# Four gate parts made during the last scan and brought back with an identity product, and a last product in two halves

## Chip, cores and metric

The kernel runs on one core of a Trainium2 chip. The metric is the device time of one execution in microseconds. Time before: 1269.98 us, the median of three runs (1269.86 to 1270.35).

## What is computed

Two layers act on x, four sequences of 1024 rows of 256 numbers, all in float32. Each layer is modulated by six vectors per sequence (shift, scale and gate of two branches). Layer 0 is a dilated attention and a linear layer whose input is quantised by blocks. Layer 1 is a selective scan (Mamba) and a recurrent gate layer. What matters here is the end of layer 1:

```python
def step(h, inp):                      # the scan, over 1024 rows
    a, bx, c = inp
    h = a * h + bx
    y = jnp.einsum('bds,bs->bd', h, c)
    return (h, y)
...
y = y + D_param[None, None, :] * x_branch
y = y * jax.nn.silu(z)
return jnp.einsum('btd,de->bte', y, c_proj_w)
...
def step(c, xt):                       # the gates, over the 4 sequences
    ft = jax.nn.sigmoid(xt @ wf.T + c @ uf.T + bf)
    it = jax.nn.sigmoid(xt @ wi.T + c @ ui.T + bi)
    gt = jnp.tanh(xt @ wc.T + c @ uc.T + bc)
    c = ft * c + it * gt
    return (c, None)
c_final, _ = lax.scan(step, c0, x)
h = jnp.tanh(jnp.einsum('tbi,oi->tbo', x, wo) + c_final @ uo.T + bo)
```

## The kernel before

The work is cut into G = 8 halves of 512 rows (two per sequence), named h ahead of their scan and g behind it. The scan of a half has 32 steps (STEPS), so the whole program has 256 scan steps, numbered m. The 32 steps are four blocks of channels (kd) of eight steps, and a step holds two states, each 128 channels by 512 rows. For step m:

- ACT makes the decays, two Exp activations of 128x512 into PSUM (`act_decay`, L1254). Banks 0 to 3 hold the states of two steps, so the decays of step m wait for DVE's product of step m - 2.
- POOL multiplies u with the loaded row of B (`pool_scan`, L1914, in odd halves with a small sum at L1920). It waits for the sum of y of step m - 4, whose buffer it takes. SP loads the rows of B and C from DRAM.
- DVE runs the recurrence over both states (`dve_scan`, L1691) and multiplies the result with the row of C (L1697).
- PE adds both halves of that product onto y with the identity (`pe_scan`, L874), in bank Y. After the eighth step DVE multiplies y with silu(z) (`dve_gate`, L1677).

The other work of the halves before and behind goes between the steps. Each engine's program is one list, put together by `in_time`: every chain yields the step at which its next piece is due (tables TIMES, or numbers at the yield), and at each quarter of a step the due pieces are emitted ahead of the scan's own part. An engine runs its list in order, and semaphores join the engines.

A gate of the recurrent layer is a product of 128x512 in two parts: `pe_gate_x` (from hA, the normalised rows; L720) and `pe_gate_c` (from the state c; L728), each two matmuls over k into one PSUM bank. There are six (f, i, c; two blocks of 128 channels each). ACT evicts a gate at L1177 (`act_gate`).

The last half (g = 7) has no scan behind it to hide in, and has chains of its own. `pe_last` makes the projection `c_proj` (L747) in two banks, the parts from c of all six gates, the transposes of the normalised rows (L458), the parts from hA, then the output's products (L784, L735). c for this half is that of half 5 (`c_of(g)`), so it is known long before. The gates' banks are LAST_GATE, and LAST_ORDER is the order in which they are made. ACT and DVE write hA's two blocks (L898 and L1386). `dve_last` has, in order: bias sums for the output (L1632, three times), `dve_sum` (L1615), the gates' arithmetic for either half of c (L1639, L1641, L1645, L1648), and the output sums (L1657 and on). `dve_final` places two more `dve_sum` at L1615 around the last gated product. `act_loads` brings in the rows of earlier halves for the output by DMAs from ACT's queue (L1200, L1203), one every two steps of the last scan.

Of the kernel before, what the change touches and what calls it, by code (L numbers as in the profile page):

```python
# [104 lines left out]
LAST_CPROJ, LAST_GATE, LAST_PX, LAST_OM = (Y0, X0), (X1, 0, 1, 2, 3, Y), (Y0, Y), 0  # L105

LAST_ORDER, LAST_TANH = (0, 2, 4, 1, 3, 5), {1: X0, 2: 2}

# [10 lines left out]
             "ffn_mm", "ffn_tmp", "res1"]  # L119
MAMBA = ["pad", "xb_mm", "xc_init", "conv", "xc", "z_mm", "z_tanh", "z_ev", "bc_mm", "bc_sb", "softplus", "spare",  # L120
         "dt_copy", "u", "dt_cut", "first_decay", "to_add"]
# [17 lines left out]
def build(nc, d):  # L139
    with ExitStack() as ctx:  # L140
# [65 lines left out]
        def cols_view(a):  # L206
# [56 lines left out]
               [rows_view(a) for a in (xb_flat[:, 0:JH * E], xb_flat[:, JH * E:2 * JH * E])] + [woT[:], xrows[(G - 1) % 3]]]  # L263
        gates1 = rowmod

        mod_d = nc.dram_tensor("mod_scratch", (B, 6, E), F32).ap()
# [456 lines left out]

        def pe_gate_c(n, bank, g, first):

            gate, mt = "fic"[n // 2], n % 2
            for k in range(KE):
                x = pe.matmul(ps[:, bank, :], gu[gate][:, k, mt * P:(mt + 1) * P], c_of(g)[:, k, :],  # L728
                              start=(first and k == 0), stop=(not first and k == KE - 1))
            return x  # L730

        def pe_px(q, bank):
            for j in (2 * q, 2 * q + 1):
                for k in range(KE):
                    x = pe.matmul(ps[:, bank, (j % 2) * E:(j % 2 + 1) * E], hA[:, k, j:TH:JH], gw["o"][:, k, :],  # L735
                                  start=(k == 0), stop=(k == KE - 1))
            x.then_inc(S.px_mm, 1)

        def pe_last():
# [4 lines left out]
            def c_proj(kd, q):  # L744
# [4 lines left out]
                return x  # L749

            for q in range(2):

                yield t + 30 + q / 2
                if q == 0:
                    pe.wait_ge(S.gated, 4 * g + KD - 1)
                    pe.wait_ge(S.cp_gated, B)
                    pe.wait_ge(S.px, 2 * g)
                else:
                    pe.wait_ge(S.fin_add, B)
                for kd in range(KD - 1):  # L760
                    c_proj(kd, q)
            yield t + 31.75
            pe.wait_ge(S.c_new, g - 1)
            pe_gate_c(LAST_ORDER[0], LAST_GATE[0], g, True)

            yield t + 32.75
            pe.wait_ge(S.gated, 4 * g + 4)
            for q in range(2):
                c_proj(KD - 1, q).then_inc(S.cp_mm, 1)
            for n in (1, 2, 3):  # L770
                pe_gate_c(LAST_ORDER[n], LAST_GATE[n], g, True)
            pe.wait_ge(S.resA, 2 * g + 2)
            pe.wait_ge(ln["ln4"].hn, 2 * g + 2)
            for k in range(KE):
                pe_transposes(hnA, k, LAST_CPROJ[k], ln["ln4"].mm)
            for n in (4, 5):
                pe_gate_c(LAST_ORDER[n], LAST_GATE[n], g, True)
            pe.wait_ge(ln["ln4"].out, 2 * g + 2)
# [84 lines left out]
        def pe_scan(step, quarter):  # L863
# [5 lines left out]
            q = quarter // 2  # L869
            if q == 0:  # L870
                pe.wait_ge(S.prod, m + 1)
                if i == 0:
                    pe.wait_ge(S.dx, 4 * g + kd + 1)
# [340 lines left out]
        def act_last():  # L1214
            g = G - 1
            yield STEPS * G + 1
            act.wait_ge(S.fin_sum, 1)
# [461 lines left out]
        def dve_scan(step, quarter):  # L1679
# [14 lines left out]
            elif quarter == 2:  # L1694
                dve.wait_ge(S.scan, m + 1)
                dve.wait_ge(crow_in[m % 3], 16 * (m // 3 + 1))
                dve.tensor_tensor(inp[:, m % RING, :, :], states_of(m), c_at[:, m % 3, :, :], ALU.mult).then_inc(S.prod, 1)  # L1697

# [286 lines left out]
```

## Time and profile before

| | |
|---|---|
| median of three runs | 1269.98 us |
| the profiled execution | 1271.65 us |
| its span, first to last instruction | 1270.1 us |
| DVE busy | 1159.2 us, 91% of the span |
| PE busy (matmuls) | 1145.3 us, 90% |
| POOL busy | 980.9 us, 77% |
| ACT busy | 794.3 us, 63% |
| mean granted TensorE clock | 0.984 |

The profile shows one execution. Lines (L1691) are those of the kernel before. Times within it count from its first instruction. An entry such as "x4" merges instructions that follow each other, and what stands in square brackets is idle time of the engine ahead of them and what ended it.

### The profile page before, as it was taken

Reading aid. Unit: us, or ns where it says so; the run is one execution under the profiler, and the core shown is the slowest. Engines: PE = TensorE matmul, PEld = TensorE weight load, DVE = VectorE, ACT = ScalarE, POOL = GpSimd, SP = SyncE. Lnnn points to the kernel's source line nnn. Section 1 sums busy time; section 2 is a strip of 40 time slices with the busy share of each in tenths; the row PEclk is TensorE's granted clock in tenths of the full one; section 3 lists DMA queues with packets and bytes.
Section 4 is the critical chain, followed back from the end, with each engine's and each line's share of the span. In section 5 each row is a group of like instructions: output and inputs, shape, how many; then the busy total and the mean of one; then the engine's idle time right before and its main releaser. Section 6 shows DMA issues by size and latency. Waiting matters only on the chain.

```text
span 1270.1 us, 12563 instructions
## 1 busy us (share of the span) xinstructions
PE 1145.3 (90%) x3612; PEld 641.0 (50%) x3612; DVE 1159.2 (91%) x1136; ACT 794.3 (63%) x1443; POOL 980.9 (77%) x711
## 2 busy tenths in 40 slices
PE   7989678998999899998999899998999899889896
PEld 4636333654457444764457444764457444443454
DVE  3868999999999999899999999899999999999987
ACT  2256567765785677855786678855786666645522
POOL 3216886889788988989778888989778896876852
PEclk9999989999999999999999999999999999989999
DMA  8308588876878677876768588866868686989922
GB/s 280 118 15 301 188 268 286 275 233 234 278 234 291 214 275 276 296 233 235 279 219 302 207 276 286 290 230 239 281 228 292 204 279 222 306 314 351 369 84 99
DMA packets 92308, 313.87 MB, mean 247 GB/s; under 512 B 10432, under 2 KB 15680, under 8 KB 91984
## 3 DMA queue, kind: packets, MB, share of 16 engines
q1 hardware_dynamic: 89936, 306.26, 70.1%
q10 hardware_dynamic: 2304, 6.82, 1.6%
q8 instruction: 28, 0.46, 0.1%
q14 instruction: 40, 0.33, 0.1%
HBM read 301.73 MB, written 11.31 MB: 246 GB/s over the span
## 4 chain that ended last, share of the span: by engine, by line
PE 46%; DVE 19%; POOL 16%; ACT 9%; issue 8%; DMA 2%; SPq 0%; DVEq 0%; POOLq 0%; ACTq 0%
PE ps L874 14%; DVE ps L1691 11%; POOL arena L1914 9%; PE ps L585 5%; PE ps L808 4%; PE ps L593 3%; PE ps L631 2%; DVE arena L1697 2%; PE ps L707 2%; PE ps L720 2%; PE ps L712 2%; PE ps L735 2%; ACT arena L898 2%; ACT ps L1254 2%; PE ps L728 1%
## 5 line engine op out<-in xcount | busy, mean ns | idle before, releaser
L1914 POOL TENSOR_TENSOR arena<-arena 128x1024 f32<-128x1024 f32 x255 | 600.7, 2364 | 139.9 <-PE ps L874 115.2
L1691 DVE TENSOR_TENSOR_SCAN ps<-ps,arena 128x1024 f32<-128x1024 f32 (+1 forms) x257 | 585.9, 2280 | 29.6 <-ACT ps L1254 16.7
L874 PE MATMUL ps<-arena,identF 128*128 128x512 f32 x1024 | 484.0, 604 | 46.7 <-DVE arena L1697 29.7
L1254 ACT ACTIVATE ps<-arena,negA 128x512 f32<-128x512 f32 x512 | 332.8, 684 | 89.6 <-DVE arena L1697 83.9
L874 PEld LDWEIGHTS ps<-arena,identF 128*128 128x128 f32 x1024 | 190.8, 193 | 266.6 <-issue 209.5
L1697 DVE TENSOR_TENSOR arena<-ps,arena 128x1024 f32<-128x1024 f32 x256 | 312.0, 1219 | 5.9
L889 ACT ACTIVATE arena<-arena,rnln 128x256 f32<-128x256 f32 x118 | 61.9, 590 | 42.5 <-POOL rnln L1724 25.7
L631 PE MATMUL ps<-arena,inw 128*128 128x512 f32 x128 | 60.0, 614 | 11.7 <-ACT arena L898 9.6
L712 PE MATMUL ps<-arena,inw 128*128 128x512 f32 x128 | 62.0, 608 | 3.3 <-DVE arena L1421 3.3
L1266 ACT ACTIVATE arena<-ps 128x2 f32<-128x2 f32 x128 | 22.1, 172 | 67.9 <-DVE arena L1697 67.4
L898 ACT ACTIVATE arena<-ps,modT 128x512 f32<-128x512 f32 x43 | 51.7, 1264 | 13.7 <-PE ps L458 11.6
L1733 POOL TENSOR_TENSOR arena<-arena 128x512 f32<-128x512 f32 x42 | 53.0, 1273 | 8.7 <-ACT arena L1074 7.1
L808 PE MATMUL ps<-cpw,arena 128*128 128x256 f32 x224 | 55.6, 402 | 2.1 <-DVE arena L1677 2.1
L808 PEld LDWEIGHTS ps<-cpw,arena 128*128 128x128 f32 x224 | 53.9, 327 | 5.7 <-DVE arena L1677 3.1
L585 PE MATMUL ps<-arena,wqT 128*128 128x128 f32 (+2 forms) x128 | 42.3, 481 | 12.4 <-ACT arena L898 8.1
L631 PEld LDWEIGHTS ps<-arena,inw 128*128 128x128 f32 x128 | 24.2, 194 | 45.9 <-issue 28.7
L458 PEld LDWEIGHTS ps<-identF,arena 128*128 128x128 f32 x256 | 30.1, 144 | 30.0 <-ACT arena L898 9.4
L1416 DVE SCALAR_TENSOR_TENSOR ps<-arena,vecs,ps 128x512 f32<-128x512 f32 x64 | 43.5, 749 | 0.8 <-ACT ps L1004 0.8
L458 PE MATMUL ps<-identF,arena 128*128 128x128 f32 x256 | 35.8, 280 | 6.4 <-ACT arena L898 3.6
L712 PEld LDWEIGHTS ps<-arena,inw 128*128 128x128 f32 x128 | 24.8, 195 | 31.7 <-issue 25.2
L593 PEld LDWEIGHTS ps<-wvT,arena 128*128 128x128 f32 x256 | 38.7, 227 | 3.5 <-issue 3.1
L585 PE MATMUL ps<-arena,wkT 128*128 128x128 f32 (+2 forms) x128 | 39.0, 454 | 1.0 <-ACT arena L1029 1.0
(219 smaller groups left out, 1715.7 us busy)
## 6 DMA issues: line engine op xcount, KB each, us to landing
arena<-bc_scratch SPq DMA_DIRECT2D x511, 512.0 KB, 5.0
arena<-in_x SPq DMA_DIRECT2D x16, 256.0 KB, 6.8
arena<-in_x SPq DMA_DIRECT2D x8, 512.0 KB, 8.9
xr_scratch<-arena SPq DMA_DIRECT2D x6, 512.0 KB, 6.7
px_scratch<-arena SPq DMA_DIRECT2D x6, 512.0 KB, 6.3
out_x<-arena SPq DMA_DIRECT2D x5, 512.0 KB, 2.6
arena<-bc_scratch SPq DMA_DIRECT2D x9, 256.0 KB, 3.7
woT<-in_woT SPq DMA_DIRECT2D x4, 512.0 KB, 9.4
```

What stands on the lines that cost most here:

```text
L458: x = pe.transpose(ps[:, bank, j * P:(j + 1) * P], src[:, j, k * P:(k + 1) * P], identF[:])
L585: x = pe.matmul(ps[:, bank, cols[0]:cols[1]], w[:, h, k, :], hB1[:, k, 0:TH:TH // (cols[1] - cols[0])], start=(k == 0), stop=(k == KE - 1))
L593: x = pe.matmul(ps[:, bank, g * P:(g + 1) * P], hB1[:, k, o * P * dil:(o + 1) * P * dil:dil], wvT[:, h, k, :], start=(k == 0), stop=(k == ...
L631: x = pe.matmul(ps[:, bank, :], inw[:, k, kd * P:(kd + 1) * P], hB3[:, k, :], start=(k == 0), stop=(k == KE - 1))
L712: x = pe.matmul(ps[:, Y0, :], inw[:, k, DI + kd * P:DI + (kd + 1) * P], hB3[:, k, :], start=(k == 0), stop=(k == KE - 1))
L808: x = pe.matmul(ps[:, Y0, (j % 2) * E:(j % 2 + 1) * E], y2T[:, kd, j:TH:JH], cpw[:, kd, :], start=(kd == 0), stop=(kd == KD - 1))
L874: x = pe.matmul(ps[:, Y, :], identF[:], inp[:, m % RING, q, :], start=False, stop=(i == BLOCK_STEPS - 1 and q == 1), skip_group_check=True)
L898: act.activation(out, src, ACT.Identity, bias=modT[:, layer_col + k, b:b + 1], scale=modT[:, layer_col + 2 + k, b:b + 1]).then_inc(ln[site ...
L1254: x = act.activation(ps[:, 2 * (m % 2) + q, :], dt[:, kd, :], ACT.Exp, scale=negA[:, kd, 2 * i + q:2 * i + q + 1])
L1691: x = dve.tensor_tensor_scan(states, states, inp[:, m % RING, q, :].rearrange("p q t -> p (q t)"), 0.0, ALU.mult, ALU.add)
L1697: dve.tensor_tensor(inp[:, m % RING, :, :], states_of(m), c_at[:, m % 3, :, :], ALU.mult).then_inc(S.prod, 1)
L1914: x = pool.tensor_tensor(inp[:, m % RING, :, :], u[:, kd:kd + 1, :].broadcast_to([P, 2, TH]), b_at[:, m % 3, :, :], ALU.mult)
```

## The change

Four of the six parts from c of the last half (LAST_SAVED: places 0, 3, 4 and 5 of the order) are made in bank X0 during the last scan, from step 235 on, one every two steps. ACT copies each to SBUF, from step 236 on, into places that are free by then (hB3 and a part of inw). Where the part stood in `pe_last`, one product with the identity now puts it back into the gate's bank; that of place 0 is due at 32.5 instead of 31.75. The semaphore c_part counts both: PE's next part waits for ACT's copy of the one before, ACT's copy for PE's part. The product of the last scan step (m = 255) is made in two instructions, and PE's two sums of y wait for one half each.

```diff
+LAST_SAVED = (0, 3, 4, 5)
...
+        c_parts = [hB3[:, 0, :], hB3[:, 1, :], inw[:, 1, 0:TH], inw[:, 1, TH:2 * TH]]
...
+        def pe_saved(e):
+            pe.matmul(ps[:, LAST_GATE[LAST_SAVED[e]], :], identF[:], c_parts[e], start=True, stop=False)
...
+            for e, n in enumerate(LAST_SAVED):
+
+                yield t + 11 + 2 * e
+                if e:
+                    pe.wait_ge(S.c_part, 2 * e)
+                else:
+                    pe.wait_ge(S.c_new, g - 1)
+                    pe.wait_ge(S.bc_sb, G)
+                    pe.wait_ge(S.xc, 4 * G)
+                pe_gate_c(LAST_ORDER[n], X0, g, True, True).then_inc(S.c_part, 1)
...
-            yield t + 31.75
-            pe.wait_ge(S.c_new, g - 1)
-            pe_gate_c(LAST_ORDER[0], LAST_GATE[0], g, True)
+            yield t + 32.5
+            pe.wait_ge(S.c_part, 2 * len(LAST_SAVED))
+            pe_saved(0)
...
-            for n in (1, 2, 3):
+            for n in (1, 2):
                 pe_gate_c(LAST_ORDER[n], LAST_GATE[n], g, True)
+            pe_saved(1)
+            pe_saved(2)
...
-            for n in (4, 5):
-                pe_gate_c(LAST_ORDER[n], LAST_GATE[n], g, True)
+            pe_saved(3)
...
-            if q == 0:
+            if m == G * STEPS - 1:
+                pe.wait_ge(S.prod, m + 1 + q)
+            elif q == 0:
                 pe.wait_ge(S.prod, m + 1)
...
+            for e in range(len(LAST_SAVED)):
+                yield STEPS * g + 12 + 2 * e
+                act.wait_ge(S.z_mm, 4 * G)
+                act.wait_ge(S.c_part, 2 * e + 1)
+                act.activation(c_parts[e], ps[:, X0, :], ACT.Copy).then_inc(S.c_part, 1)
...
-                dve.tensor_tensor(inp[:, m % RING, :, :], states_of(m), c_at[:, m % 3, :, :], ALU.mult).then_inc(S.prod, 1)
+
+                for q in (slice(0, 2),) if m < G * STEPS - 1 else (slice(0, 1), slice(1, 2)):
+                    dve.tensor_tensor(inp[:, m % RING, q, :], states_of(m)[:, q, :], c_at[:, m % 3, q, :], ALU.mult).then_inc(S.prod, 1)
```

How the instructions stand on the engines, at three places (the changed kernel's lines are numbered anew: L720 is L724 there, L728 is L732, L747 is L754, L874 is L894, L1177 is L1197, L1254 is L1279).

ACT in the last scan, from the eviction of hA's second block on, before (L1254 are the decays, L1177 is the first gate's eviction):

```order
L1254 ACTIVATE ps<-arena,negA 128x512 [waits prod]
L1254 ACTIVATE ps<-arena,negA 128x512
L1200 DMA arena<-px_scratch 128x1024 [waits px_out]
L1254 ACTIVATE ps<-arena,negA 128x512 [waits prod]
L1254 ACTIVATE ps<-arena,negA 128x512
L1177 ACTIVATE arena<-ps,vecs 128x512 [waits g_mm,c_new]
L1254 ACTIVATE ps<-arena,negA 128x512 [waits prod]
L1254 ACTIVATE ps<-arena,negA 128x512
```

And in the changed kernel:

```order
L1279 ACTIVATE ps<-arena,negA 128x512 [waits prod]
L1279 ACTIVATE ps<-arena,negA 128x512
L1240 ACTIVATE arena<-ps 128x512 [waits c_part,z_mm]
L1220 DMA arena<-px_scratch 128x1024 [waits px_out]
L1279 ACTIVATE ps<-arena,negA 128x512 [waits prod]
L1279 ACTIVATE ps<-arena,negA 128x512
L1197 ACTIVATE arena<-ps,vecs 128x512 [waits g_mm,c_new]
L1279 ACTIVATE ps<-arena,negA 128x512 [waits prod]
L1279 ACTIVATE ps<-arena,negA 128x512
L1240 ACTIVATE arena<-ps 128x512 [waits c_part,z_mm]
L1223 DMA arena<-xr_scratch 128x1024 [waits xr_out]
L1279 ACTIVATE ps<-arena,negA 128x512 [waits prod]
```

The copies of the first and the second part (L1240) stand behind the decays of steps 236 and 238 and ahead of those of steps 237 and 239 and of a load; the first gate's eviction follows the decays of step 237.

PE at the same place, before (guf and gwf are the weights of the f gate, cT is c, prod is the product of DVE):

```order
L720 MATMUL ps<-arena,gwf 128x512
L728 MATMUL ps<-cT,guf 128x512 [waits c_new]
L728 MATMUL ps<-cT,guf 128x512
L874 MATMUL ps<-arena,identF 128x512 [waits prod]
L874 MATMUL ps<-arena,identF 128x512
L874 MATMUL ps<-arena,identF 128x512 [waits prod]
L874 MATMUL ps<-arena,identF 128x512
L720 MATMUL ps<-arena,gwf 128x512 [waits g_ev]
L720 MATMUL ps<-arena,gwf 128x512
L728 MATMUL ps<-cT,guf 128x512 x2
```

And in the changed kernel:

```order
L724 MATMUL ps<-arena,gwf 128x512
L732 MATMUL ps<-cT,guf 128x512 [waits c_new]
L732 MATMUL ps<-cT,guf 128x512
L732 MATMUL ps<-cT,guf 128x512 [waits xc,bc_sb,c_new]
L732 MATMUL ps<-cT,guf 128x512
L894 MATMUL ps<-arena,identF 128x512 [waits prod]
L894 MATMUL ps<-arena,identF 128x512
L894 MATMUL ps<-arena,identF 128x512 [waits prod]
L894 MATMUL ps<-arena,identF 128x512
L724 MATMUL ps<-arena,gwf 128x512 [waits g_ev]
L724 MATMUL ps<-arena,gwf 128x512
L732 MATMUL ps<-cT,guf 128x512 x2
```

The first saved part stands behind the first gate and ahead of the sums of y of steps 234 and 235.

PE at the end of the last scan, from the sums of step 254 on, before:

```order
L874 MATMUL ps<-arena,identF 128x512 [waits prod]
L874 MATMUL ps<-arena,identF 128x512
L728 MATMUL ps<-cT,guf 128x512 [waits c_new]
L728 MATMUL ps<-cT,guf 128x512
L874 MATMUL ps<-arena,identF 128x512 [waits prod]
L874 MATMUL ps<-arena,identF 128x512
L747 MATMUL ps<-cpw,arena 128x256 [waits gated]
L747 MATMUL ps<-cpw,arena 128x256 x3
L728 MATMUL ps<-cT,gui 128x512 x2
L728 MATMUL ps<-cT,guc 128x512 x2
L728 MATMUL ps<-cT,guf 128x512 x2
```

And in the changed kernel:

```order
L894 MATMUL ps<-arena,identF 128x512 [waits prod]
L894 MATMUL ps<-arena,identF 128x512
L894 MATMUL ps<-arena,identF 128x512 [waits prod]
L744 MATMUL ps<-arena,identF 128x512 [waits c_part]
L894 MATMUL ps<-arena,identF 128x512 [waits prod]
L754 MATMUL ps<-cpw,arena 128x256 [waits gated]
L754 MATMUL ps<-cpw,arena 128x256 x3
L732 MATMUL ps<-cT,gui 128x512 x2
L732 MATMUL ps<-cT,guc 128x512 x2
L744 MATMUL ps<-arena,identF 128x512
L744 MATMUL ps<-inw,identF 128x512
```

The first gate's part is gone from between the sums of steps 254 and 255, and the product with the identity that replaces it stands between the two sums of step 255. Behind the projection two parts and two identity products stand where three parts stood.

## Rows read from the trace of the kernel before

**Rows 1.** Groups of the last scan, 1140 to 1228 us: busy, mean ns | idle before.
```profile
L1691 DVE TENSOR_TENSOR_SCAN ps<-ps,arena 128x1024 f32<-128x1024 f32 x22 | 50.3, 2288 | 0.4 <-POOL arena L1920 0.4
...
L1697 DVE TENSOR_TENSOR arena<-ps,arena 128x1024 f32<-128x1024 f32 x23 | 28.1, 1223 | 0.7
L1254 ACT ACTIVATE ps<-arena,negA 128x512 f32<-128x512 f32 x42 | 27.3, 682 | 31.4 <-DVE arena L1697 31.2
```
**Rows 2.** The chain of waits after the scan: start, us, what.
```profile
1240.42 10.31 PE ps L720 x24
```
**Rows 3.** Timeline, the gates after the scan: start, us, engine, line.
```profile
1236.82 1.88 PE L728 MATMUL ps<-cT,gui 128*128 128x512 f32 x4
1237.02 1.20 DVE L1386 TENSOR_SCALAR arena<-ps,modT 128x512 f32<-128x512 f32 x1 [1.90 <-PE ps L458]
...
1240.26 1.88 PE L720 MATMUL ps<-arena,gwf 128*128 128x512 f32 x4
...
1242.95 0.69 DVE L1639 SCALAR_TENSOR_TENSOR arena<-arena,cT 128x512 f32<-128x512 f32 x1 [0.28 <-ACT arena L1177]
...
1251.48 0.69 DVE L1645 SCALAR_TENSOR_TENSOR arena<-arena 128x512 f32<-128x512 f32 x1 [2.28 <-ACT arena L1177]
```
**Rows 4.** Timeline, the last step of the scan, and two halves elsewhere.
```profile
1223.92 1.88 PE L728 MATMUL ps<-cT,guf 128*128 128x512 f32 x4
...
1223.98 1.22 DVE L1697 TENSOR_TENSOR arena<-ps,arena 128x1024 f32<-128x1024 f32 x1
...
1225.13 2.22 DVE L1615 TENSOR_TENSOR arena<-arena 128x1024 f32<-128x1024 f32 x1
...
1225.63 1.88 PE L874 MATMUL ps<-arena,identF 128*128 128x512 f32 x4
...
1227.62 0.69 DVE L1677 TENSOR_TENSOR arena<-ps,arena 128x512 f32<-128x512 f32 x1 [0.28 <-PE ps L874]
...
1258.71 1.28 DVE L1670 TENSOR_TENSOR arena<-ps,bias_rows 128x512 f32<-128x512 f32 x2
```
**Rows 5.** Timeline of PE in the last scan.
```profile
1146.23 1.98 PE L720 MATMUL ps<-arena,gwf 128*128 128x512 f32 x4 [1.36 <-ACT arena L898]
...
1149.77 3.60 PE L874 MATMUL ps<-arena,identF 128*128 128x512 f32 x8
...
1173.40 5.71 PE L874 MATMUL ps<-arena,identF 128*128 128x512 f32 x12
```
**Rows 6.** Timeline of ACT and DVE in the last scan.
```profile
1148.80 1.30 ACT L1254 ACTIVATE ps<-arena,negA 128x512 f32<-128x512 f32 x2 [1.53 <-DVE arena L1697]
...
1152.15 2.29 DVE L1691 TENSOR_TENSOR_SCAN ps<-ps,arena 128x1024 f32<-128x1024 f32 x1
...
1155.73 1.30 ACT L1254 ACTIVATE ps<-arena,negA 128x512 f32<-128x512 f32 x2 [2.16 <-DVE arena L1697]
...
1159.07 2.29 DVE L1691 TENSOR_TENSOR_SCAN ps<-ps,arena 128x1024 f32<-128x1024 f32 x1
...
1199.72 0.57 ACT L1173 ACTIVATE arena<-ps 128x512 f32<-128x512 f32 x1
```
**Rows 7.** Timeline of POOL and of the scans that follow it.
```profile
1175.42 2.35 POOL L1914 TENSOR_TENSOR arena<-arena 128x1024 f32<-128x1024 f32 x1 [1.40 <-PE ps L874]
...
1179.20 2.35 POOL L1914 TENSOR_TENSOR arena<-arena 128x1024 f32<-128x1024 f32 x1 [1.15 <-DMA arena<-bc_scratch]
...
1186.52 0.19 POOL L1920 TENSOR_TENSOR arena<-arena 128x2 f32<-128x2 f32 x1
...
1187.37 2.29 DVE L1691 TENSOR_TENSOR_SCAN ps<-ps,arena 128x1024 f32<-128x1024 f32 x1
...
1192.76 2.36 POOL L1914 TENSOR_TENSOR arena<-arena 128x1024 f32<-128x1024 f32 x1 [0.88 <-DMA arena<-bc_scratch]
...
1205.77 2.30 DVE L1691 TENSOR_TENSOR_SCAN ps<-ps,arena 128x1024 f32<-128x1024 f32 x1 [0.40 <-POOL arena L1920]
```
**Rows 8.** Timeline, PE at a lower clock.
```profile
1125.20 3.78 PE L712 MATMUL ps<-arena,inw 128*128 128x512 f32 x4 [3.27 <-DVE arena L1421]
```

More of the change, by code:

```diff
@@ L119 @@
              "ffn_mm", "ffn_tmp", "res1"]
-MAMBA = ["pad", "xb_mm", "xc_init", "conv", "xc", "z_mm", "z_tanh", "z_ev", "bc_mm", "bc_sb", "softplus", "spare",
+MAMBA = ["pad", "xb_mm", "xc_init", "conv", "xc", "z_mm", "z_tanh", "z_ev", "c_part", "bc_mm", "bc_sb", "softplus", "spare",
          "dt_copy", "u", "dt_cut", "first_decay", "to_add"]
@@ L722, in pe_gate_x, with pe_gate_c @@
             return x
-        def pe_gate_c(n, bank, g, first):
+        def pe_gate_c(n, bank, g, first, alone=False):
             gate, mt = "fic"[n // 2], n % 2
@@ L728, in pe_gate_c @@
                 x = pe.matmul(ps[:, bank, :], gu[gate][:, k, mt * P:(mt + 1) * P], c_of(g)[:, k, :],
-                              start=(first and k == 0), stop=(not first and k == KE - 1))
+                              start=(first and k == 0), stop=((alone or not first) and k == KE - 1))
             return x
```

## Prediction

> **What bounds the kernel now.** I read the groups of the last scan first, then the chain of waits, and then the timeline of the last 125 us in pieces. In the last scan it is DVE that has no idle time: 22 scans of 2288 ns and 23 products of 1223 ns stand with 1.1 us of idle time before them in 88 us [rows 1]. A scan step therefore lasts 3.46 us (the scans at 1152.15 and 1159.07 are those of steps 237 and 239, counted back from the last, 255, [rows 6]). After the scan the chain goes through PE: the 24 records of the six gate products from hA take 10.31 us in one piece [rows 2]. Every float32 matmul of the program shows as two records, and they follow each other every 0.43 us, so one product of 128x512 holds PE for 0.86 us and one gate part (two products) for 1.72 us (eight records, two parts, fill 1236.82 to 1240.26, [rows 3]). A group's own duration is about 0.16 us more than that, the drain of its last matmul.
>
> **The tail, after the scan.** hA is complete when DVE's L1386 ends at 1237.02 + 1.20 = 1238.22, but PE is then in the parts from c of the last two gates, and the products from hA start only at 1240.26 [rows 3]. The change puts one identity product (0.86 us, ends at 1236.82 + 0.86 + 0.16 = 1237.84) where these 3.43 us stood. PE then waits for DVE and starts at about 1238.32, plus 0.1 us for a start from idle (four records last 1.98 after a wait [rows 5] and 1.88 without): 1238.42. Term: **-1.84 us**. Does it reach the end? DVE is ready for the first gate at 1242.95 at the earliest, because its bias sums come first [rows 3]; before it was only just late there. That holds up the first half of c a little, but the last gate's eviction decides: L1645 at 1251.48 stands right behind it, and DVE has only some 5 us of work from 1242.7 on (five operations of 0.43 to 0.69 and the sum L1615, 1.22) before it needs that eviction, at 1249.6 with the change. So the 1.84 us go through to the end, where all later work follows L1645.
>
> Ahead of that the change swaps parts of equal place: behind c_proj two parts and two identity products (3.43 + 1.72 us) stand where three parts stood (5.15 us), so nothing changes there.
>
> **The last product in two halves.** In the trace DVE's product ends at 1225.20, PE is busy with the first gate's part from 1223.92 and starts the last two y sums at 1225.63; the gated product follows at 1227.62 [rows 4]. Split, the halves end at about 1224.65 and 1225.26 (two instructions of 128x512 take 1.28 us together, [rows 4], against 1.22). The first y sum can start at 1224.71 and takes 0.96 with its idle start. Then comes the first saved part's identity product, 0.86, and only then the second y sum: 1224.71 + 0.96 + 0.86 + 0.86 + 0.16 = 1227.55, against 1225.63 + 1.88 = 1227.51 before. Term: **0**. The bounds: the half's release could be 0.1 later, and nothing could come out better than -0.27, since DVE's own L1615 lasts until 1227.35 and the gated product stands behind it [rows 4]. The Trainium skill says the opposite of a zero here (Perfetto Trace Analysis, Optimizing Scalar/DVE Operations): breaking up an instruction that causes bubbles elsewhere may let work end sooner. By it the half sum would start 0.55 us earlier and the sum of my terms would be up to 0.27 us lower; the order of PE's rows above takes that back.
>
> **The scan, where the parts now are made.** Four parts are 4 x 1.72 = 6.9 us of PE and four evictions of 128x512 are 4 x 0.57 us of ACT (L1173's 0.57, [rows 6]). ACT has 31 us of idle time there [rows 1] and pays this easily. What it does not have is freedom of order: the eviction stands ahead of the decay activations of the next scan step, and it waits for PE. I walk the first:
>
> PE has done the gate part at 1149.77 [rows 5] and makes the first saved part until 1149.77 + 1.88 = 1151.65. ACT arrives at 1148.80, where the decays of the scan at 1152.15 start now [rows 6]. With the eviction ahead of them they start at 1151.65 + 0.09 + 0.53 = 1152.27, and as two of them take 1.30 they end at 1153.57. The scan starts at 1153.62 instead of 1152.15. **+1.47 us**, on the engine that never idles.
>
> The second: PE does the first part, two y sums, the second gate and the second part in one run, 1149.77 + 1.72 + 3.43 + 3.43 + 1.72 = 1160.07, drained at 1160.23. ACT would start the decays of the scan now at 1159.07 at 1155.73 + 1.47 = 1157.20; behind the eviction they start at 1160.85 and end at 1162.15. The scan starts at 1162.18 instead of 1159.07 + 1.47 = 1160.54: **+1.64 us**.
>
> The third: PE is through at 1165.38, the decays behind that eviction end at 1167.3 and their scan is due at 1169.7, so no stall. The fourth: PE is through at 1173.96, the decays end at 1175.87, due at 1176.6, 0.7 us to spare. Both terms are 0.
>
> If ACT's wait did not hold the decays behind it, both stalls would go. The Trainium skill states that ACT and DVE are strict FIFO (TensorE: Matmul & The Clock Gate, Architectural detail); by that the sum has the 3.1 us, without it -1.8 remains. The trace before has no eviction that waits in this place, so it cannot say.
>
> **What PE's backlog does next.** Between 1149.77 and the y sum of step 241 at 1173.40 [rows 5] PE has 7 y sums and 6 gate parts, 22.33 us, and 1.3 us idle. With 6.87 us more that sum starts at 1178.97, 5.57 later, while DVE is 3.11 later. POOL's product at 1175.42 waits for this sum [rows 7], so it comes at 1180.97. It is the first of four such operations of 2.36 up to 1186.71, the end of L1920 there; a wait of 1.15 us for a row lies between them at 1179.20 and absorbs that much [rows 7], so the four now end at about 1191.07, 4.36 later. The scan behind it, at 1187.37 now, is due at 1187.37 + 3.18 = 1190.55: **+0.6 us**, the last bit with what the scan before it lost. From there to the scan at 1205.77, which now waits 0.40 us for POOL, POOL is shifted by 4.35 or by less, as it also waits 0.88 for a row at 1192.76 [rows 7]. If that wait vanishes, because the row's transfer had three microseconds more to land, POOL comes 3.5 later, and DVE's shift falls from 3.7 to that: -0.2. If it stays, the shift grows to 4.35: +0.6. I take -0.2, since every stall of the scan gives the transfers time.
>
> **The sum.** 1.47 + 1.64 + 0.6 - 0.2 + 0 - 1.84 = **+1.7 us**. The profiled execution took 1271.65 us (span 1270.1); with the change 1273.35. The median of the runs is 1269.98, 1.67 below the profiled one, so I forecast 1271.7. The bounds around it are -0.2 to +0.8 for POOL, -0.27 to +0.1 for the halves and 0.3 either way for the two stalls together, so this case reaches from 1270.9 to 1272.9. No change in a measurement of this kernel is within 0.2%, 2.54 us.
>
> **Rivals.**
> *The waits hide (0.2).* PE makes the parts soon enough, or ACT gets its decays out in time. For it: each decay pair has 2.05 us to spare now (it ends at 1150.10, the scan starts at 1152.15). Against it: PE has no idle time from 1146.23 until well behind the second gate [rows 5]. Only the tail's terms stay: -1.84 to -2.1, 1267.9 to 1268.2.
>
> *Clearly slower (0.13): POOL decides from the eleventh step on.* Place: the products between 1175 and 1206. It decides once PE's lag over DVE exceeds one POOL wait, which by my walk it just does. If rows land later too, POOL keeps 4.35 us and adds half a microsecond to each of two row waits, and the 0.7 us of the fourth eviction is used up: scan loss 4.35 + 1.0 + 0.5 = 5.8, less 1.84: +4, 1274.0.
>
> *The split works after all (0.03):* on top of the first rival 0.27 us; it changes no sign.
>
> *PE's clock (0.02).* PE now stands still for some 0.6 us before the gate products and 0.8 us before the last y sums. In this trace four records took 3.78 instead of 1.88 us after 3.27 us of standing still [rows 8]; a stretch of six to eight such records in the gate products would cost 3 to 4 us. A pause of 0.6 us has no such row.
>
> **Chances.** My case has 0.62, the first rival 0.2 with the split's 0.03 beside it, the slower ones 0.15. Above 1272.5 lie a fifth of my case (0.12) and the slower rivals (0.15 less what stays below, 0.12): slower 0.24. Faster by more than 2.54 us needs the first rival and something I have not seen: 0.04. Same 0.72. The range takes in the first rival and the main case with its bounds and the nearer part of the slower one: 1267.8 to 1273.8.
>
> **What would show it.** Right: the first two evictions behind the parts wait for PE by 2.9 and 4.8 us, DVE's scans of steps 237 and 239 show about 1.5 us of idle time each, released by ACT; DVE's L1615 and the y sums end as before relative to the last product; the products from hA start right after DVE's column activation, some 1.8 us sooner relative to the last scan. Wrong: no idle time of DVE in the last scan block (then the first rival), or idle times released by POOL that sum to over 1 us (then the slower one), or a granted clock under 1.00 in the gate products.

## The result, and the profile after

| | before | changed |
|---|---|---|
| median of the runs, us | 1269.98 (1269.25 to 1271.85, 11 runs) | 1274.12 (1271.80 to 1275.34, 11 runs) |
| ratio to before | | 1.0028, 95% interval 1.0019 to 1.0036 |
| profiled execution, us (span) | 1271.65 (1270.1) | 1274.12 (1272.6) |
| granted clock of TensorE, mean | 0.984 | 0.983 |

The kernel became slower by 0.28%, more than the 0.2% that the prediction counts as no change, though the interval begins at 0.19%. The forecast was 1271.7 with a range from 1267.8 to 1273.8. The ratio gives 1.0028 x 1269.98 = 1273.5 us, inside the range but above the prediction's main case, which ended at 1272.9; the plain median of the changed kernel's runs lies 0.3 us above the range. Of the three outcomes the one with 0.24 came true, not the one with 0.72. Profiled execution against profiled execution the difference is 2.47 us, where the terms gave 1.7.

The first view is that of the groups in the last scan, which answers to [rows 1] (busy, mean ns | idle before, and the releasers).

```profile
L1716 DVE TENSOR_TENSOR_SCAN ps<-ps,arena 128x1024 f32<-128x1024 f32 x22 | 50.4, 2290 | 4.6 <-ACT ps L1279 3.0 <-POOL arena L1947 1.6
L1941 POOL TENSOR_TENSOR arena<-arena 128x1024 f32<-128x1024 f32 x21 | 49.5, 2359 | 21.6 <-PE ps L894 19.5 <-DMA arena<-bc_scratch 2.0
```

DVE's 22 scans (L1716 now) had 0.4 us of idle time and have 4.6 now: 3.0 behind ACT and 1.6 behind POOL. The waits of the stretch 1140 to 1230 us say who held ACT and POOL (total us, times, longest).

```profile
POOL arena L1941 <- PE ps L894: 19.5, 6, 7.0
...
ACT arena L1240 <- PE ps L732: 9.5, 2, 5.0
...
ACT inw L1240 <- PE ps L732: 2.6, 2, 1.5
...
POOL arena L1941 <- DMA arena<-bc_scratch: 2.0, 3, 0.7
```

The copies of the parts (L1240) wait 12.1 us for PE in all, and POOL waits 19.5 us for PE's sums of y, where 11.0 stood before in the same stretch. The timeline shows the places (start, us, engine, line).

```profile
1147.95 3.60 PE L732 MATMUL ps<-cT,guf 128*128 128x512 f32 x8
...
1151.65 0.60 ACT L1240 ACTIVATE arena<-ps 128x512 f32<-128x512 f32 x1 [4.47 <-PE ps L732]
...
1152.14 1.29 ACT L1279 ACTIVATE ps<-arena,negA 128x512 f32<-128x512 f32 x2
...
1153.53 2.30 DVE L1716 TENSOR_TENSOR_SCAN ps<-ps,arena 128x1024 f32<-128x1024 f32 x1 [1.41 <-ACT ps L1279]
...
1156.54 3.60 PE L732 MATMUL ps<-cT,guf 128*128 128x512 f32 x8
...
1160.23 0.60 ACT L1240 ACTIVATE arena<-ps 128x512 f32<-128x512 f32 x1 [5.00 <-PE ps L732]
...
1160.72 2.51 ACT L1279 ACTIVATE ps<-arena,negA 128x512 f32<-128x512 f32 x4
...
1162.12 2.30 DVE L1716 TENSOR_TENSOR_SCAN ps<-ps,arena 128x1024 f32<-128x1024 f32 x1 [1.56 <-ACT ps L1279]
```

This is the first term, as walked against [rows 6]. PE makes the gate's part and the first saved part in one run, 1147.95 to 1151.55. The copy that stood ready since 1147.18 starts at 1151.65, the two decays behind it at 1152.14, and the scan 1.41 us late. With the second part the same comes again, 5.00 us of waiting and a scan 1.56 us late. The scan of step 239 that started at 1159.07 starts at 1162.12, 3.05 later. The timeline of the later part of the scan, in two pieces, POOL's backlog and the last step:

```profile
1180.88 2.35 POOL L1941 TENSOR_TENSOR arena<-arena 128x1024 f32<-128x1024 f32 x1 [2.52 <-PE ps L894]
...
1191.01 2.30 DVE L1716 TENSOR_TENSOR_SCAN ps<-ps,arena 128x1024 f32<-128x1024 f32 x1 [0.45 <-POOL arena L1947]
...
1196.87 2.35 POOL L1941 TENSOR_TENSOR arena<-arena 128x1024 f32<-128x1024 f32 x1 [0.73 <-DMA arena<-bc_scratch]
...
1200.05 2.36 POOL L1941 TENSOR_TENSOR arena<-arena 128x1024 f32<-128x1024 f32 x1 [0.56 <-DMA arena<-bc_scratch]
...
1210.15 2.30 DVE L1716 TENSOR_TENSOR_SCAN ps<-ps,arena 128x1024 f32<-128x1024 f32 x1 [1.13 <-POOL arena L1947]
```

```profile
1228.36 1.29 DVE L1724 TENSOR_TENSOR arena<-ps,arena 128x512 f32<-128x512 f32 x2
...
1229.11 1.12 PE L894 MATMUL ps<-arena,identF 128*128 128x512 f32 x2 [0.64 <-DVE arena L1724]
...
1230.07 1.02 PE L744 MATMUL ps<-arena,identF 128*128 128x512 f32 x2
...
1230.93 1.02 PE L894 MATMUL ps<-arena,identF 128*128 128x512 f32 x2
...
1232.06 0.69 DVE L1702 TENSOR_TENSOR arena<-ps,arena 128x512 f32<-128x512 f32 x1 [0.32 <-PE ps L894]
```

Against [rows 7]: POOL's product behind the first late sum starts at 1180.88 instead of 1175.42 (walked: 1180.97), and the scan of step 247 (at 1187.37 before) waits 0.45 us for POOL. Then come two waits of POOL for rows, 0.73 and 0.56 us, and the scan of step 252 waits 1.13 us, where it waited 0.40. It starts at 1210.15 instead of 1205.77: 4.38 us late.

In the second piece, against [rows 4], the gated product starts 3.70 us after the last product (3.64 before). The tail in the timeline:

```profile
1241.25 1.02 PE L744 MATMUL ps<-inw,identF 128*128 128x512 f32 x2
1241.45 1.18 DVE L1411 TENSOR_SCALAR arena<-ps,modT 128x512 f32<-128x512 f32 x1 [1.89 <-PE ps L462]
...
1242.69 1.98 PE L724 MATMUL ps<-arena,gwf 128*128 128x512 f32 x4 [0.42 <-DVE arena L1411]
...
1247.00 0.69 DVE L1664 SCALAR_TENSOR_TENSOR arena<-arena,cT 128x512 f32<-128x512 f32 x1
...
1254.01 0.69 DVE L1670 SCALAR_TENSOR_TENSOR arena<-arena 128x512 f32<-128x512 f32 x1 [2.28 <-ACT arena L1197]
```

Against [rows 3]: the products from hA start right behind DVE's L1411, 10.63 us after the gated product instead of 12.64. From there to DVE's last operation behind a gate it takes 11.32 us (1242.69 to 1254.01) where it took 11.22. DVE comes to the first gate later after them than before (4.31 us instead of 2.69, to 1247.00), since its bias sums stand ahead, and has made that good at the last gate, for which it waits 2.28 us as before. In the chain of waits their 24 records stand as before in one piece, 10.58 us long where [rows 2] has 10.31. Counted from the start in [rows 3], 1240.26, it was 10.47 before; the other 0.1 us is the start from idle.

```profile
1242.69 10.58 PE ps L724 x24
```

Laid end to end: 1.41 + 1.56 (ACT), 0.45 (step 247), 0.73 more at step 252 and 0.23 in small pieces are the 4.38 us; 0.06 at the halves make 4.44 at the gated product; less 2.01 in the tail leaves 2.43 at the products from hA, and 2.47 at the end.

### The profile page after: what moved, and what is told of

Read it like the earlier page. It is cut to its first block, busy times and chain, and to the rows that moved or that the text cites. A ratio compares the mean times of both kernels' runs of the same rounds, so it can differ in the third digit from the quotient of the medians.

```text
span 1272.6 us, 12589 instructions
## 1 busy us (share of the span) xinstructions
PE 1148.1 (90%) x3620; PEld 642.5 (50%) x3620; DVE 1156.2 (91%) x1137; ACT 795.9 (63%) x1447; POOL 980.6 (77%) x711
## 4 chain that ended last, share of the span: by engine, by line
PE 45%; DVE 19%; POOL 16%; ACT 9%; issue 8%; DMA 3%; SPq 0%; DVEq 0%; POOLq 0%; ACTq 0%
PE ps L894 14%; DVE ps L1716 10%; POOL arena L1941 9%; PE ps L589 5%; PE ps L826 4%; PE ps L597 3%; DVE arena L1724 2%; PE ps L635 2%; ACT ps L1279 2%; ACT arena L918 2%; PE ps L711 2%; PE ps L724 2%; PE ps L716 2%; PE ps L739 2%; DMA arena<-bc_scratch 2%
## 5 line engine op out<-in xcount | busy, mean ns | idle before, releaser
L1716 DVE TENSOR_TENSOR_SCAN ps<-ps,arena 128x1024 f32<-128x1024 f32 (+1 forms) x257 | 585.9, 2280 | 35.0 <-ACT ps L1279 21.0
L894 PE MATMUL ps<-arena,identF 128*128 128x512 f32 x1024 | 483.8, 603 | 45.1 <-DVE arena L1724 28.4
L1279 ACT ACTIVATE ps<-arena,negA 128x512 f32<-128x512 f32 x512 | 332.6, 683 | 78.5 <-DVE arena L1724 73.5
L894 PEld LDWEIGHTS ps<-arena,identF 128*128 128x128 f32 x1024 | 191.0, 194 | 264.3 <-issue 209.7
L1724 DVE TENSOR_TENSOR arena<-ps,arena 128x1024 f32<-128x1024 f32 (+1 forms) x257 | 312.1, 1215 | 5.9
L724 PE MATMUL ps<-arena,gwf 128*128 128x512 f32 x64 | 30.9, 605 | 10.0 <-ACT arena L918 9.6
```

Of the source, the lines that this page charges most:

```text
L894: x = pe.matmul(ps[:, Y, :], identF[:], inp[:, m % RING, q, :], start=False, stop=(i == BLOCK_STEPS - 1 and q == 1), skip_group_check=True)
L1279: x = act.activation(ps[:, 2 * (m % 2) + q, :], dt[:, kd, :], ACT.Exp, scale=negA[:, kd, 2 * i + q:2 * i + q + 1])
L1716: x = dve.tensor_tensor_scan(states, states, inp[:, m % RING, q, :].rearrange("p q t -> p (q t)"), 0.0, ALU.mult, ALU.add)
L1724: dve.tensor_tensor(inp[:, m % RING, q, :], states_of(m)[:, q, :], c_at[:, m % 3, q, :], ALU.mult).then_inc(S.prod, 1)
```

## The experiments

Every kernel was timed in five rounds beside the kernel before on the same chip; the ratios are to those runs, with their 95% interval. Diffs are against the changed kernel.

**The tail alone.**

```diff
-                pe_gate_c(LAST_ORDER[n], X0, g, True, True).then_inc(S.c_part, 1)
...
-                act.activation(c_parts[e], ps[:, X0, :], ACT.Copy).then_inc(S.c_part, 1)
```

> Leaves out: the four parts from c and their copies are never made, so the identity products bring back old contents of the buffers; the tail's instructions are those of the change. Theory 1 (the scan side costs, the tail side gains): against the kernel before -1.9 us (0.15%), the scans of the last block as before, no idle time of DVE released by ACT, the products from hA 1.9 to 2.1 us sooner after the last gated product. Rival (the tail costs too, for instance by the split product or a lower clock): 0 or above.

Measured: 1269.37 us, ratio 0.9984 (0.9975 to 0.9992), 2.0 us below before. No scan of the last block waits for ACT or POOL, and the products from hA come 10.60 us after the gated product. The tail's term holds in the time as in the trace. POOL's row waits ahead of step 252, which matter below, come to 1.46 us here and reach no scan.

**The scan alone:** parts made and copied, tail as before.

```diff
-            pe_saved(0)
+            pe_gate_c(LAST_ORDER[0], LAST_GATE[0], g, True)
...
-            pe_saved(1)
-            pe_saved(2)
-            pe_saved(3)
+            for n in (4, 5):
+                pe_gate_c(LAST_ORDER[n], LAST_GATE[n], g, True)
```

> The four parts are made and copied during the scan as in the change, but the tail makes all six parts anew, as before; only the last product stays in two halves. Theory 1: +4.4 us against the kernel before (the shift of the last scans in the profile of the change), with two idle times of DVE of 1.4 and 1.6 us released by ACT and two of 0.5 and 1.1 released by POOL; about 2 us above the change. Rival (part of the change's time comes from the tail): less than +4.

Measured: 1277.52, ratio 1.0050 (1.0038 to 1.0063). The two stalls behind ACT are 1.41 and 1.57, that of step 247 is 0.45, and that of step 252 is twice the change's:

```profile
1210.20 2.30 DVE L1715 TENSOR_TENSOR_SCAN ps<-ps,arena 128x1024 f32<-128x1024 f32 x1 [2.33 <-POOL arena L1946]
```

So making the parts costs 6.4 us by the ratio (4.8 to 8.0 by its interval), more than the 4.4 expected. In its profiled execution the wait of step 252, which I had sized by a guess, is 1.2 us longer than in the change's; what remains above the expectation lies within the interval.

**The copies one scan step later.**

```diff
-                yield STEPS * g + 12 + 2 * e
+                yield STEPS * g + 13 + 2 * e
```

> ACT's four copies stand one scan step later, behind the decays they held up. Theory A (the order on ACT is the cause of the loss): the two idle times of DVE released by ACT vanish and nothing takes their place; 3.0 us less than the change, so about 1 us above or below the kernel before. Theory P (PE has no room for 6.9 us there): the sums of y are as late as in the change relative to PE and later relative to DVE, POOL waits for them, and DVE now waits for POOL: walked through the rows of before, idle times of about 0.5 us at step 238, 1.6 at 240, 1.0 at 245 and 0.6 at 247; the same time as the change within 0.7 us.

Measured: 1274.55, ratio 1.0028 (1.0016 to 1.0040), the same as the change. The waits of DVE's scans in its timeline (steps 238, 240, 245, 247 and 252), and one of its product with silu(z):

```profile
1153.21 2.30 DVE L1716 TENSOR_TENSOR_SCAN ps<-ps,arena 128x1024 f32<-128x1024 f32 x1 [0.49 <-POOL arena L1947]
...
1161.82 2.30 DVE L1716 TENSOR_TENSOR_SCAN ps<-ps,arena 128x1024 f32<-128x1024 f32 x1 [1.59 <-POOL arena L1947]
...
1165.96 0.69 DVE L1702 TENSOR_TENSOR arena<-ps,arena 128x512 f32<-128x512 f32 x1 [0.59 <-PE ps L894]
...
1180.68 2.30 DVE L1716 TENSOR_TENSOR_SCAN ps<-ps,arena 128x1024 f32<-128x1024 f32 x1 [0.18 <-POOL arena L1947]
...
1188.16 2.30 DVE L1716 TENSOR_TENSOR_SCAN ps<-ps,arena 128x1024 f32<-128x1024 f32 x1 [0.46 <-POOL arena L1947]
...
1208.29 2.30 DVE L1716 TENSOR_TENSOR_SCAN ps<-ps,arena 128x1024 f32<-128x1024 f32 x1 [2.12 <-POOL arena L1947]
```

No scan waits for ACT any more, and nothing is won: the scans one step later, 238 and 240 in place of 237 and 239, wait for POOL (0.49, 1.59), POOL having waited for PE's sums, which stand behind the parts, and DVE waits another 0.59 us for PE's sums themselves. ACT's place in the order was the form of the stall. What was short is PE's room in front of the sums: 6.9 us of work put into a stretch in which PE had 1.3 us idle.

**The change again.**

> The changed kernel itself, beside the others on one chip. If the third wait for POOL (step 252, 1.13 us in the first profile, 2.3 and 2.1 in two experiments, 0.2 in a third) depends on when the row transfers land and not on the kernel, it shows another value here while the waits at steps 237, 239 and 247 show 1.41, 1.56 and 0.45 again. Ratio to before 1.0028 within its interval.

Measured: 1273.65, ratio 1.0022 (1.0013 to 1.0031); its stalls are 1.41, 1.56, 0.46 and, at step 252, 0.80.

**Two parts instead of four,** made at the same places.

```diff
-LAST_SAVED = (0, 3, 4, 5)
+LAST_SAVED = (4, 5)
```

> Only the parts of places 4 and 5 are saved, made in the first two places of the change; places 0 and 3 as before. The cost by PE's room: half of the added PE time (3.4 us). Walk: the two idle times released by ACT (1.4 and 1.6 us) stay, since they come from the first two parts; PE's lag at step 241 is 2.1 instead of 5.6 us, so POOL's 0.45 us at step 247 goes. Tail: the products from hA start after two identity products, 0.2 us later than in the change. Sum against before: +3.0 + (0 to 1 at step 252) - 1.75 = +1.3 to +2.3 us. Theory A (every part costs its copy's wait only) gives the same; a rival that the cost is by number of parts gives half of the change's, +0 to +0.3.

Measured: 1272.22, ratio 1.0011 (1.0002 to 1.0020), +1.4 us, at the lower end of what was expected. The two waits behind ACT are 1.41 and 1.56 again. The third and fourth part cause no stall where they are made; they cost what POOL lags later (step 247 is at 0 here, step 252 at 0.50).

**The parts where PE stands idle.** The first is made in the 1.36 us for which PE waits for ACT's L898 ahead of the first gate [rows 5]; the last stands ahead of the output's first product, where PE waits 2.31 us for ACT in the kernel before:

```profile
1196.98 2.24 PE L735 MATMUL ps<-gwo,arena 128*128 128x256 f32 x8 [2.31 <-ACT arena L1177]
```

```diff
+            if g == G - 2:
...
+                pe_gate_c(LAST_ORDER[LAST_SAVED[0]], X0, G - 1, True, True).then_inc(S.c_part, 1)
...
+                yield t + (24.75,)[e - 1]
...
-                yield STEPS * g + 12 + 2 * e
+                yield STEPS * g + (12, 26)[e]
```

> The same two parts, made where PE stands idle in the trace of before: the first between the transposes of hA and the first gate of the half before (1.36 us idle at 1146.23), the second ahead of the first output product (2.31 us idle at 1196.98). Theory P: PE loses 0.4 us at most, no idle time of DVE is released by ACT, and POOL's stay under 0.5 us; the tail's gain of 1.75 us comes through: -1.5 to -1.8 us against before. Rival (any added work in the last scan costs, for instance through ACT's copies or the shared bank): 0 or above.

And with a third part, ahead of the sums of step 244:

```diff
-LAST_SAVED = (0, 3, 4, 5)
+LAST_SAVED = (3, 4, 5)
...
+                yield t + (21, 24.75)[e - 1]
```

> Places 3, 4 and 5 saved, the third part ahead of the sums of step 244 (1.48 us idle at 1180.58), the others as in the version with two. PE loses 0.4 + 0.3 us. The products from hA start as in the change, 0.2 us sooner than with two. -1.7 to -2.0 us against before; the rival that the third place costs: -1.3 or above.

Measured: two parts 1268.86, ratio 0.9985 (0.9976 to 0.9994); three parts 1269.52, ratio 0.9985 (0.9976 to 0.9994). Both are faster than the kernel before, by about 1.9 us, which is under the 0.2% counted as no change but has intervals wholly below 1, and so faster than both kernels compared here. PE in the last scan with three parts:

```profile
1143.51 1.88 PE L732 MATMUL ps<-cT,guf 128*128 128x512 f32 x4
1145.23 1.88 PE L724 MATMUL ps<-arena,gwf 128*128 128x512 f32 x4
1146.95 1.88 PE L732 MATMUL ps<-cT,guf 128*128 128x512 f32 x4
1148.67 3.60 PE L895 MATMUL ps<-arena,identF 128*128 128x512 f32 x8
```

The first saved part (1143.51) fills the idle time, and the first gate follows it without a gap. The sums of y at 1148.67 start 0.1 us later than before against DVE's scans, and no scan waits for ACT or POOL. The waits of POOL sum to 16.4 us, where before there were 17.0 (11.0 for PE, 6.0 for rows):

```profile
POOL arena L1942 <- PE ps L895: 13.2, 5, 5.4
...
POOL arena L1942 <- DMA arena<-bc_scratch: 3.2, 4, 1.2
```

**The last product whole,** twice.

```diff
-                for q in (slice(0, 2),) if m < G * STEPS - 1 else (slice(0, 1), slice(1, 2)):
+                for q in (slice(0, 2),):
```

> The last product in one instruction again, the rest as in the change. My walk: the same as the change within 0.1 us, and rather sooner: with the product whole, the first sum starts 0.6 us later but the identity product and both sums then run without the wait; the last sum ends at about 1225.26 + 0.1 + 3 x 0.86 = 1227.9 in the clock of before instead of 1227.55: +0.35 us at most. Rival (the split is what gains in the tail): +0.6 us or more.

> The change with the last product whole, once more. Halves worth nothing (the prediction's term): ratio as the change, 1.0022 to 1.0028, and the gated product starts 3.6 to 3.75 us after the last product, as with halves. If the whole product costs the 0.0012 to 0.0018 that its first measurement was above the change: 1.0040 again. The mean of a spread of over 2 us between executions would give anything between.

Measured: 1276.30, ratio 1.0040 (1.0026 to 1.0054), and 1275.98, ratio 1.0036 (1.0024 to 1.0048). The trace of the second, at the last step:

```profile
1227.47 1.22 DVE L1722 TENSOR_TENSOR arena<-ps,arena 128x1024 f32<-128x1024 f32 x1
...
1228.75 1.12 PE L892 MATMUL ps<-arena,identF 128*128 128x512 f32 x2 [1.18 <-DVE arena L1722]
...
1229.71 1.02 PE L744 MATMUL ps<-arena,identF 128*128 128x512 f32 x2
...
1230.57 1.02 PE L892 MATMUL ps<-arena,identF 128*128 128x512 f32 x2
...
1231.70 0.69 DVE L1700 TENSOR_TENSOR arena<-ps,arena 128x512 f32<-128x512 f32 x1 [0.55 <-PE ps L892]
```

The gated product starts 4.23 us after the last product (4.22 in the first run) where halves have 3.70. In the changed order the halves are worth 0.53 us, and I had expected at most 0.35: with the product whole, the identity product of the saved part still stands between the two sums and puts the second off by 0.86. The expectation had that product in it, but left out the 0.16 us of the last matmul's drain, which is contained in the 1227.55 it compares with; with it the walk gives 0.55. The change's zero at this place is a cost of about a half microsecond by that order, and its recovery by the halves. The times point the same way, though their intervals overlap with the change's.

The same in the kernel with three parts in the gaps, where gate 0's part stands ahead of both sums:

> Three parts in PE's gaps, the last product whole. In this kernel gate 0's part stands ahead of the last sums of y as in the kernel before. Halves worth nothing: 0.9985 again. If halves matter: there they could save at most 0.27 us, 0.0002, so 0.9987 at the most; and the gated product stands 3.6 to 3.9 us after the start of the last product.

Measured: 1269.39, ratio 0.9987 (0.9979 to 0.9996). The gated product starts 3.63 us after the last product, with halves 3.64. There the halves are worth nothing.

**A fourth row buffer.**

```diff
-                    sp.wait_ge(S.inp, m - 2)
+                    sp.wait_ge(S.inp, m - 2 if m < FOURTH + 3 else m - 3)
```

> The change, with a fourth buffer for the rows that POOL multiplies in its last 18 steps (from step 238 on), so that a row's transfer is released by POOL's product four steps back instead of three. Theory R (a row's transfer starts when POOL's own product three steps back has ended, so POOL's delay of over four microseconds passes unabsorbed through the row waits, and each row wait adds to it; over the runs so far the stall of step 252 is POOL's row waits at 1192 to 1201 us added up, less 0.1 to 0.2): these two row waits (0.73 and 0.56 in the change, 0.58 and 0.39 in its repeat) are gone and the stall of step 252, 1.13 and 0.80 there, falls to under 0.2; the stall of step 247 stays at 0.45 and the two behind ACT at 1.4 and 1.56. Time 0.8 to 1.1 us below the change: ratio to the kernel before about 1.0018 instead of 1.0022 to 1.0028. The prediction's step (the transfer has more time when the scan is late) as rival: the fourth buffer changes nothing, row waits of 0.3 to 1.2 remain since the rows land late for want of bandwidth.

> Three parts in PE's gaps with the fourth row buffer. There POOL's row waits (0.84 at 1191 us) cause no stall of DVE, so theory R says no difference: ratio 0.9985 again, within 0.0005. If rows land late for want of bandwidth instead, again no difference. Only a cost of the additional buffer itself would show here, as a ratio over 0.999.

Measured: 1272.49, ratio 1.0016 (1.0006 to 1.0027), whose interval holds the 1.0022 of the change's second measurement and overlaps with that of the first; and 1269.58, ratio 0.9993 (0.9983 to 1.0003). The ratios don't decide, so the traces have to. POOL and DVE of the first:

```profile
1197.20 2.37 POOL L1954 TENSOR_TENSOR arena<-arena 128x1024 f32<-128x1024 f32 x1 [0.34 <-DMA arena<-bc_scratch]
...
1200.62 2.37 POOL L1954 TENSOR_TENSOR arena<-arena 128x1024 f32<-128x1024 f32 x1 [0.78 <-DMA arena<-bc_scratch]
...
1210.74 2.30 DVE L1729 TENSOR_TENSOR_SCAN ps<-ps,arena 128x1024 f32<-128x1024 f32 x1 [0.98 <-POOL arena L1960]
```

The row waits are still there, 0.34 and 0.78, and step 252 still waits 0.98. Below is the time from issue to landing of the rows for POOL, issued between 1186 and 1200 us; first in the changed kernel, then with the fourth buffer.

```profile
DMA to landing us min/median/max: 5.8/6.4/7.3
```

```profile
DMA to landing us min/median/max: 7.1/8.4/8.9
```

The issue of the row of step 250, before, in the change and with the fourth buffer:

```profile
1186.74 0.32 SPq L447 DMA_DIRECT2D arena<-bc_scratch  x1
```

```profile
1191.00 0.32 SPq L451 DMA_DIRECT2D arena<-bc_scratch  x1
```

```profile
1188.22 0.43 SPq L464 DMA_DIRECT2D arena<-bc_scratch  x1
```

In the change POOL could start its product at 1196.87; with the fourth buffer the row was issued 2.8 us sooner (3.5 us sooner against DVE's scans, which stand 0.74 us later in that execution) and POOL started at 1197.20, which against the scans is 0.4 us sooner. So almost all of the earlier issue went into a longer way to landing. The transfers of this stretch move 356 GB/s with the fourth buffer and 339 in the changed kernel, with the DMA engines nine tenths busy in most slices. My theory of the release fell, and the row waits are what the rival beside it named. That bandwidth is its reason is argued from these rates and not shown by a run: with the fourth buffer SP also issues each row for POOL about 0.4 us behind a row of C for DVE, and no run keeps the two apart. In the second kernel (three parts in the gaps) the profiled execution has row waits of 1.81 and 1.92 us and a stall of 2.50 at step 252, which the same kernel without the fourth buffer does not have, and its ratio is over the 0.999 that I had named as a sign of a cost of the buffer. Its interval overlaps with that of 0.9985, so the cost is not shown.

What did hold is the sum rule. POOL's two row waits between 1192 and 1201 us, added up, against the stall of step 252 in the seven profiled executions in which four parts are made at or after the change's places:

| kernel | row waits, us | stall of step 252, us |
|---|---|---|
| scan alone | 2.47 | 2.33 |
| copies later | 2.26 | 2.12 |
| the change | 1.29 | 1.13 |
| fourth row buffer | 1.12 | 0.98 |
| the change again | 0.97 | 0.80 |
| product whole, second | 0.79 | 0.60 |
| product whole, first | 0.30 | 0.20 |

The stall is the sum of the row waits less 0.10 to 0.19. Before, 1.14 us of row waits (0.88 and 0.26) made a stall of 0.40 [rows 7]; with three parts in the gaps 0.84 made none, and in the tail alone 1.46 made none. Scan alone and the first measurement of the product whole have the same instructions up to step 252 and ran on the same chip, and their row waits are 2.47 and 0.30: that spread is not the kernel's.

## Where the prediction was right, and which step failed

**The first two evictions (+1.47, +1.64).** Right: 1.41 and 1.56, at the steps named, with ACT's waits of 4.47 and 5.00 where "2.9 and 4.8" stood (the first now counts from the end of the decays). The rule that decided here, cited as strict FIFO from the Trainium skill (TensorE: Matmul & The Clock Gate, Architectural detail), agrees with the trace: the decays stood ready behind the copy and did not pass it.

**The third and fourth eviction (0).** Right: the copies wait 1.54 and 1.09 us for PE and no scan behind them waits.

**PE's backlog (+0.6 at step 247).** Right as a walk: POOL's product 1180.88 against 1180.97, the stall 0.45.

**Step 252 (-0.2).** This is the step that failed: "I take -0.2, since every stall of the scan gives the transfers time". The stall grew by 0.73 in the profiled execution of the change, so the term was mis-sized by 0.93 us, more than the whole miss of 0.77 between the profiled executions. Both POOL terms together were forecast at +0.4 with bounds of -0.2 and +0.8 around that; they measured 0.45 + 0.73 = 1.18, just inside. The branch that the prediction walked and did not take, "If it stays, the shift grows to 4.35", is what came: 4.38. The reason behind it was wrong in two ways. A row's transfer is released by POOL's own product three steps back, so a late POOL issues late: the row of step 250 was issued at 1191.00, 4.3 us later than before. And where a fourth buffer took that tie away, the row landed only 0.4 us sooner against the scans for an issue 3.5 us sooner, so time given to these transfers was hardly any use. How large the two row waits are differs from execution to execution (0.30 to 2.47 in sum), and with four parts nearly all of it reaches the scan; before, about two thirds of it was absorbed.

**The tail (-1.84).** Right in place, 0.17 short: -2.01.

**The halves (0).** Right in the sum (+0.06), and by the account given there: the order of PE's products takes back what the half sum gains. The runs add the size, 0.53. The page that it set against its zero, the Trainium skill's Perfetto Trace Analysis, Optimizing Scalar/DVE Operations, says "may" and speaks of engines that aren't saturated; here breaking up the product gained 0.53 us in the one order and 0.01 in the other.

**The base.** The forecast translated a difference of profiled executions to medians, by 1.67 us. The change's profiled execution lies at its own median, so the ratios say more (1.0028 and 1.0022 are 3.6 and 2.8 us) than the profiles (2.5). The 2.5 us lie within both intervals, so no remainder is shown. Much of the difference between single executions arises ahead of the place of the change: the scan of step 237 is due (its wait behind ACT taken off) between 1149.2 and 1152.9 us in the fourteen profiled executions. From there to the end of the span it is 118.0 us before and 120.5 and 120.2 in the two executions of the change, 2.5 and 2.2 more.

**Rivals.** That the waits hide fell with the first stall. That POOL decides, priced at +4, was half right: its sign, "idle times released by POOL that sum to over 1 us", is there with 1.58 us, and it is 2.8 in the scan alone and 4.8 with the copies later. Its other part, an exhausted reserve at the fourth eviction, did not occur. The result (+3.6 and +2.8 us by the ratios, +2.5 by the profiles) lies between my case's +1.7 and the rival's +4. So my case had the right mechanism and too small a size, and that the time fell into the range is owed to the part of it that was lent by the slower rival. I gave that rival 0.13 because I took a wait that varies by over 2 us for one that shrinks. No clock loss: the mean is 0.983, the granted clock from 1242.70 to 1253.30 us is 1.00, and the gate products take 10.58 us for 24 records.

## What to carry over

Work taken out of a tail pays only if it goes where its engine is idle: four of these parts cost 6.4 us of scan (by the ratio) inside a full stretch of PE, and three of them, placed where PE stood idle, made no scan wait. Look first for the gap, then for what stands in order behind the moved work on every engine that handles it. When a wait on transfers lies in the path of a delayed engine, ask who releases the transfer and whether it lands sooner when it is issued sooner, and size the term by the spread between executions, not by one. An item put between two halves of a dependent pair (here an identity product between two sums) takes back what splitting their producer wins.

## What the runs showed that was not expected

A row of 512 KB lands 5.8 to 7.3 us after its issue in the changed kernel and 7.1 to 8.9 with one more buffer: more loads under way made each slower, at 339 and 356 GB/s, and POOL's two row waits stayed at 1.12 us in sum (1.29 and 0.97 without the buffer). The Trainium skill (Perfetto Trace Analysis, Engine Utilization) gives about 435 GB/s as what the 16 DMA engines of one core can move together; single slices of 0.35 us reach 468 with the fourth buffer, and the means stay under the figure.

The sum of the two row waits varied from 0.30 to 2.47 us between the seven profiled executions of the table (3.73 with three parts in the gaps and the fourth buffer), and between two executions of one and the same kernel from 0.30 to 0.79. The term that I sized from one execution, with bounds 1.0 us apart, has a spread of its own of about twice that.
